# Attention's first rows in two halves, its output sums begun while probabilities are turned, routing steps spread, and the stages on either side reordered

## What is computed

```
x = x + gate * mamba(norm(x))        # layer 0: projections, a scan over 16 states, W_out
x = x + gate * moe8(norm(x))         # layer 0: 8 experts, the 2 best for each row
x = x + gate * attention(norm(x))    # layer 1: 8 heads of 128, causal softmax, T = 1024
x = x + gate * moe16(norm(x))        # layer 1: 16 experts, 2 best, at most 640 rows each

scores = q k^T / sqrt(128), masked; probs = softmax(scores)
out    = (probs v) for each head, times Wo, summed over the 8 heads
```

## Time and profile before

| | |
|---|---|
| time, 3 runs | 2908.6 us median, 2907.63 to 2910.3 |
| the profiled execution | 2909.66 us, span 2907.9 us |
| busy, share of the span | PE 86%, DVE 72%, ACT 45%, POOL 42% |
| idle time of PE in the attention steps | 31.9 us between 1405 and 2515 us |
| the chain that ended last | from the boundary at 2585.59 us, nearly all PE |

### The profile page before, as it was taken

One profiled execution on the slowest core, in us unless ns is written; L12 is line 12 of the kernel. 1 busy time (PEld: TensorE's weight loads), 2 busy tenths in 40 slices (PEclk: granted clock), 3 DMA queues, 4 the chain that ended last, 5 costly groups with the idle time before them and its releaser, 6 DMA issues. The chain is left out here.

```text
span 2907.9 us, 39192 instructions
## 1 busy us (share of the span) xinstructions
PE 2492.8 (86%) x12341; PEld 1792.0 (62%) x12342; DVE 2103.6 (72%) x4277; ACT 1296.4 (45%) x2563; POOL 1234.4 (42%) x531
## 2 busy tenths in 40 slices
PE   6677867868766759998799999999999999959998
PEld 4355545645545559998466666666666666647776
DVE  4999999999999566665666567766776677655554
ACT  4677677677665235554243324332433243311111
POOL 2799999999999036666000000020002000223344
PEclk8889989889986879999899999999999999969999
DMA  4645555555556254334300010001001000035554
GB/s 147 192 154 186 178 174 186 176 171 192 165 180 206 81 173 64 64 63 61 114 1 1 1 48 1 1 31 34 1 1 34 15 1 1 30 112 128 129 130 74
DMA packets 150845, 268.98 MB, mean 92 GB/s; under 512 B 18316, under 2 KB 107324, under 8 KB 150172
## 3 DMA queue, kind: packets, MB, share of 16 engines
q1 hardware_dynamic: 121916, 227.12, 24.3%
q0 software_dynamic: 28224, 37.78, 7.7%
q10 hardware_dynamic: 544, 2.10, 0.2%
HBM read 209.52 MB, written 57.43 MB: 92 GB/s over the span
## 5 line engine op out<-in xcount | busy, mean ns | idle before, releaser
L765 POOL TENSOR_TENSOR dbx<-u,b_all 128x2048 f32<-128x2048 f32 x128 | 578.6, 4535 | 71.2 <-DVE u L844 33.3
L1805 POOL DMA_INDIRECT slots<-at_r_rows,slot_of x64 | 62.7, 980 | 1140.3 <-DVE slot_of L2220 1048.5
L649 ACT ACTIVATE da_ps<-delta,a_neg 128x512 f32<-128x512 f32 x512 | 347.9, 689 | 132.7 <-DVE hc L917 124.5
L2066 ACT COPY at_pt<-at_pt_ps 128x512 f32<-128x512 f32 (+3 forms) x384 | 171.7, 483 | 504.5 <-PE at_pt_ps L1935 501.1
L469 PE MATMUL y_ps<-ident,hc 128*128 128x128 f32 x1536 | 246.5, 305 | 87.6 <-DVE hc L917 87.0
L1924 PE MATMUL at_s_ps<-at_qk 128*128 128x512 f32 (+3 forms) x768 | 291.4, 489 | 3.1 <-DVE at_v L2269 3.1
L1948 PE MATMUL at_o_ps<-at_pt,at_v 128*128 128x512 f32 (+3 forms) x768 | 288.6, 487 | 0.3 <-issue 0.3
L469 PEld LDWEIGHTS y_ps<-ident,hc 128*128 128x128 f32 x1536 | 200.6, 158 | 143.0 <-DVE hc L917 115.4
L2055 ACT ACTIVATE at_probs<-at_s_ps,at_small 128x128 f32<-128x128 f32 (+7 forms) x256 | 192.2, 751 | 202.2 <-DVE at_small L2280 198.9
L917 DVE TENSOR_TENSOR hc<-da_ps,c_all 128x512 f32<-128x512 f32 x384 | 257.7, 673 | 0.0
L907 DVE TENSOR_TENSOR_SCAN da_ps<-da_ps,state,dbx 128x512 f32<-128x512 f32 x192 | 243.4, 1277 | 4.5 <-ACT da_ps L649 3.6
...
...
## 6 DMA issues: line engine op xcount, KB each, us to landing
b_all<-bc_rows SPq DMA_DIRECT2D x128, 512.0 KB, 4.4
c_all<-bc_rows SPq DMA_DIRECT2D x128, 512.0 KB, 5.1
e_w<-L_ffn_w SPq DMA_DIRECT2D x32, 512.0 KB, 5.5
...
e_xs<-slots SPq DMA_DIRECT2D x16, 650.0 KB, 7.1
...
sums<-x SPq DMA_DIRECT2D x8, 512.0 KB, 6.9
```

Source lines behind the costliest of these rows:

```text
L649: nc.scalar.activation(da_ps[s % RING_DA][:], delta[:, c % 2, m, :], ACT.Exp, scale=sh.a_neg[:, m, n:n + 1]).then_inc(S["da_ready"], 1)
L765: nc.gpsimd.tensor_tensor(dbx[:, at % RING_DBX], pair, rows, ALU.mult).then_inc(S["dbx_ready"], 1)
L2066: nc.scalar.copy(pt[i // CT][:, half * CT:half * CT + m, at], pt_ps[half][:, 0:m, :]).then_inc(S[f"copied{half}"], 1)
```

## The change

1. **Scan.** The last chunk's output sums go to the freed banks da_ps[0] and [1]. Identity and the first two of four products of row tile 0 and 1 are put behind steps 61 and 62 of 64, those of tiles 2 and 3 behind the last `turn_back`. Behind POOL's gate two products a tile are left.
2. **Start of attention.** The first sequence's mods (256 KB) are loaded first, then both halves of x and `more`. All other loads wait until these have landed. DVE adds the first half in one instruction, POOL the second. Statistics, variance, root and rows are done for tiles 0 to 3 and then for 4 to 7. PE turns 4 tiles through two banks (`qk_ps`, `o_ps`), makes the three pieces of the first half, turns the other 4 tiles, and makes the other three pieces. PE waits for w_o, gate_w and the constants only at the end of the first batch.
3. **Every batch.** The pieces of head 0 come in the order q, k, v of the first half, then of the second. A bank waits for the output tile that used it, not for all eight. score(0) waits for five pieces, the sixth is awaited at step 4. The products over heads 0 to 6 of output tiles 0 and 1 are put into steps N and N + 1, ahead of turn(62) and turn(63); head 7 is added where the sums stood.
4. **Routing and next rows.** Weights move to step 50, ranks stay in 53, `slots` is parted: 5 instructions in step 54, 8 in 55. NORM moves from 53 to 55, so rows are normalised in steps 55 to 62; PE still turns them in 56 to 63. POOL's scatter is paced one step later.
5. **End of attention.** `w_qkv` is free once the last piece is made. The gates and the weights of experts 0 and 1 (2.5 MB) are loaded into its place then. `phase_experts1` starts with `e_xs` of expert 0, waits until it has landed, and loads that of expert 1.

Lines that were added or taken away, with common indentation removed and declarations left out:

```diff
@@ -481,6 +481,29 @@
+def last_first_blocks(j):
+    pair, i = j // 2, j % 2
+    if i == 0:
+        pe.wait_ge(S["hc_ready"], hc_at(LAST, STEPS - RING_DA + pair) + 1)
+        pe.wait_ge(S["y_gated"], LAST * HALVES + 1)
+        pe.wait_ge(S["w_ready"], B)
+    out = da_ps[pair][:, i * E:(i + 1) * E]
+    nc.tensor.matmul(out, sh.ident[:], sh.x[:, LAST * CT + j, :], start=(i == 0), stop=False, skip_group_check=True)
+    for k in range(2):
+        nc.tensor.matmul(out, u[:, LAST % 2, k, j * P:(j + 1) * P], sh.w_out[:, k, :], start=False, stop=False, skip_group_check=True)
+def last_blocks(pair):
+    if pair == 0:
+        pe.wait_ge(S["y_gated"], CHUNKS * HALVES)
+    for i in range(2):
+        j = pair * 2 + i
+        for k in range(2, MD):
+            mm = nc.tensor.matmul(da_ps[pair][:, i * E:(i + 1) * E], u[:, LAST % 2, k, j * P:(j + 1) * P], sh.w_out[:, k, :],
+                                  start=False, stop=(k == MD - 1), skip_group_check=True)
+    mm.then_inc(S["out_done"], 1)
@@ -500,6 +523,8 @@
+if c == LAST and k >= STEPS - 3 and k < STEPS - 1:
+    last_first_blocks(k - STEPS + 3)
@@ -524,9 +549,11 @@
-    turn_back(CHUNKS - 1, m)
+    turn_back(LAST, m)
+for j in range(2, CT):
+    last_first_blocks(j)
-    out_product(CHUNKS - 1, pair)
+    last_blocks(pair)
@@ -664,7 +691,8 @@
-nc.scalar.copy(sh.x[:, tile:tile + 2, :], proj_ps[pair][:].rearrange("p (i e) -> p i e", i=2)).then_inc(S["out_added"], 1)
+bank = da_ps[pair] if c == CHUNKS - 1 else proj_ps[pair]
+nc.scalar.copy(sh.x[:, tile:tile + 2, :], bank[:].rearrange("p (i e) -> p i e", i=2)).then_inc(S["out_added"], 1)
@@ -1498,15 +1525,14 @@
-sp.dma_start(sh.mods[:, 2], d["mod_rows"][1, 5].partition_broadcast(P)).then_inc(mods_in, 16)
-    if not early(e, 2):
-        sp.wait_ge(y_done, (e - 1) * S1)
+    if early(e, 2):
+        return
+    sp.wait_ge(y_done, (e - 1) * S1)
@@ -1516,6 +1542,7 @@
+sp.wait_ge(x_in[0], 16)
@@ -1723,8 +1751,8 @@
-SLOTS = (RANK, RANK + 1, RANK + 2)
-NORM, TURN, COPY = N - 11, N - 8, N - 7
+SLOTS = (RANK - 2, RANK + 1, RANK + 2, RANK + 3)
+NORM, TURN, COPY = N - 9, N - 8, N - 7
@@ -1735,13 +1763,16 @@
+sp.dma_start(sh.mods[:, 0:2, 0, :], d["mod_rows"][1, 0:2, 0].partition_broadcast(P)).then_inc(S["mods0_in"], 16)
-load_mods(sp, d, sh, 1, 0, S["mods_in"])
+sp.wait_ge(x_first[1], 32)
+sp.dma_start(pos[:], d["posT"]).then_inc(S["pos_in"], 16)
+sp.dma_start(sh.mods[:, 0:2, 1:B, :], d["mod_rows"][1, 0:2, 1:B].partition_broadcast(P)).then_inc(S["mods_in"], 16)
+sp.dma_start(sh.mods[:, 2], d["mod_rows"][1, 2].partition_broadcast(P)).then_inc(S["mods_in"], 16)
-sp.dma_start(pos[:], d["posT"]).then_inc(S["pos_in"], 16)
@@ -1767,8 +1798,17 @@
+sp.wait_ge(S["qk_done"], B * HEADS * PIECES + 1)
+sp.dma_start(sh.gates[:], d["mod_rows"][1, 5].partition_broadcast(P)).then_inc(sh.gates_in, 16)
+for e in range(2):
+    sp.dma_start(sh.w1[:, e], d["L1_ffn_w1"][e].rearrange("(k p) f -> p k f", p=P)).then_inc(sh.w1_in[e], 16)
+    sp.dma_start(sh.w2[:, e], d["L1_ffn_w2"][e].rearrange("(m p) f -> p m f", p=P)).then_inc(sh.w2_in[e], 16)
+sp.wait_ge(sh.gates_in, 16)
+for e in range(2):
+    sp.wait_ge(sh.w1_in[e], 16)
+    sp.wait_ge(sh.w2_in[e], 16)
@@ -1795,12 +1835,16 @@
+pool.wait_ge(x_first[1], 32)
+nc.gpsimd.tensor_tensor(sh.x[:, late], sh.x[:, late], more[:, late], ALU.add).then_inc(first_summed[1], 1)
-            pool.wait_ge(S["scored"], (rb + 1) * N + SLOTS[2] + 1 + j)
+            pool.wait_ge(S["scored"], (rb + 1) * N + SLOTS[3] + 1 + j)
@@ -1817,9 +1861,12 @@
+FIRST_PIECES = (0, 2, 4, 1, 3, 5)
+first_turned = (qk_ps, o_ps)
-    return qk_ps[:] if h else bank(i)
+    return qk_ps[:] if h else bank(FIRST_PIECES.index(i))
@@ -1828,15 +1875,19 @@
-pe.wait_ge(S["w_o_in"], 16)
-    pe.wait_ge(S["h_copied"], nb * TPB + j + 1)
+    out = qk_ps
+    if isinstance(nb, int) and nb == 0:
+        out = first_turned[j % 2]
+        pe.wait_ge(S["h_copied"], max(j, 1))
+    else:
+        pe.wait_ge(S["h_copied"], nb * TPB + j + 1)
-        last = nc.tensor.transpose(qk_ps[:, k * P:(k + 1) * P], rows[:, j % 4, k * P:(k + 1) * P], sh.ident[:])
+        last = nc.tensor.transpose(out[:, k * P:(k + 1) * P], rows[:, j % 4, k * P:(k + 1) * P], sh.ident[:])
@@ -1890,19 +1941,27 @@
-pe.wait_ge(S["gate_in"], 16)
-pe.wait_ge(S["consts_ready"], 12)
-for j in range(TPB):
+for j in range(CT):
-        if h > 0:
+        if h > 1 or i > 0:
-        elif i >= 4:
-            pe.wait_ge(S["qk_ready"], b * (HEADS * PIECES) + i - 2)
+        else:
+            pe.wait_ge(S["qk_ready"], b * (HEADS * PIECES) + h * PIECES + i)
+        products(h, i, out)
+    def project_first(place):
+        if place >= 4:
+            pe.wait_ge(S["qk_ready"], b * (HEADS * PIECES) + place - 2)
+        elif not first_batch:
+            pe.wait_ge(S["out_added"], b * TPB + place - 2)
+        products(0, FIRST_PIECES[place], bank(place))
+    def products(h, i, out):
@@ -1916,7 +1975,9 @@
-    pe.wait_ge(S["qk_ready"], b * (HEADS * PIECES) + h * PIECES + (4 if h else PIECES) + 1)
+    pe.wait_ge(S["qk_ready"], b * (HEADS * PIECES) + h * PIECES + (4 if h else PIECES - 1) + 1)
+if n == CT:
+    pe.wait_ge(S["qk_ready"], b * (HEADS * PIECES) + PIECES + 1)
@@ -1949,18 +2010,24 @@
-def output(t):
+def output(t, heads=range(HEADS)):
-    for h in range(HEADS):
+    for h in heads:
-    last.then_inc(S["out_done"], 1)
+    if HEADS - 1 in heads:
+        last.then_inc(S["out_done"], 1)
+if first_batch:
+    pe.wait_ge(S["h_copied"], CT + 1)
+    for place in range(PIECES // 2):
+        project_first(place)
+    for j in range(CT, TPB):
+        turn_rows(0, j)
-pe.wait_ge(S["out_added"], b * TPB + 1)
-for i in range(PIECES):
-    project(0, i)
+for place in range(PIECES // 2 if first_batch else 0, PIECES):
+    project_first(place)
@@ -1970,6 +2037,14 @@
+if n >= N:
+    if n == N:
+        if first_batch:
+            pe.wait_ge(S["w_o_in"], 16)
+            pe.wait_ge(S["gate_in"], 16)
+            pe.wait_ge(S["consts_ready"], 12)
+        pe.wait_ge(S["exp_done"], b * N + N - 1)
+    output(n - N, range(HEADS - 1))
@@ -1992,9 +2067,8 @@
-    pe.wait_ge(S["exp_done"], b * N + N - 1)
-output(t)
+output(t, range(HEADS - 1, HEADS))
@@ -2038,11 +2112,17 @@
+    turned = first_turned[j % 2] if isinstance(nb, int) and nb == 0 else qk_ps
-                   qk_ps[:, 0:KE * P].rearrange("p (k t) -> p k t", k=KE)).then_inc(S["h_copied"], 1)
-root(0)
-for j in range(TPB):
+                   turned[:, 0:KE * P].rearrange("p (k t) -> p k t", k=KE)).then_inc(S["h_copied"], 1)
+act.wait_ge(S["first_var"], 1)
+nc.scalar.activation(sh.var[:, 0:CT], sh.var[:, 0:CT], ACT.Sqrt).then_inc(S["first_std"], 1)
+for j in range(CT):
+    copy_rows(0, j)
+act.wait_ge(S["var_ready"], 1)
+nc.scalar.activation(sh.var[:, CT:TPB], sh.var[:, CT:TPB], ACT.Sqrt).then_inc(S["std_ready"], 1)
+for j in range(CT, TPB):
@@ -2205,15 +2282,20 @@
+def slot_sums(rb, k):
+    v = nc.vector
+    for source, dst in ((cand, slot), (rank, valid)):
+        linked(rb, v.tensor_tensor(scores[:], mask[:, k], source[:], ALU.mult))
+        linked(rb, v.tensor_reduce(dst[:, k], scores[:], AX_X, ALU.add))
+def slots_begun(rb):
+    dve.wait_ge(S["rank_taken"], rb + 1)
+    linked(rb, nc.vector.tensor_tensor(cand[:], rank[:], offs[:].rearrange("p (o e) -> p o e", o=1).broadcast_to([P, TPB, NE]), ALU.add))
+    slot_sums(rb, 0)
-    dve.wait_ge(S["rank_taken"], rb + 1)
-    linked(rb, v.tensor_tensor(cand[:], rank[:], offs[:].rearrange("p (o e) -> p o e", o=1).broadcast_to([P, TPB, NE]), ALU.add))
-    for k in range(2):
-        for source, dst in ((cand, slot), (rank, valid)):
-            linked(rb, v.tensor_tensor(scores[:], mask[:, k], source[:], ALU.mult))
-            linked(rb, v.tensor_reduce(dst[:, k], scores[:], AX_X, ALU.add))
+    slot_sums(rb, 1)
@@ -2245,20 +2327,46 @@
-for j in range(TPB):
-    stats(0, j)
-variance(0)
-invert(0)
-dve.wait_ge(S["mods_in"], 16)
-for j in range(TPB):
-    normalise_rows(0, j)
+early = slice(0, CT)
+dve.wait_ge(x_first[0], 32)
+nc.vector.tensor_tensor(sh.x[:, early], sh.x[:, early], more[:, early], ALU.add).then_inc(first_summed[0], 1)
+first_link = link_on(dve, S["first_chain"])
+def first_rows(th, var_ready, std_ready, rstd_ready):
+    dve.wait_ge(first_summed[th], 1)
+    at = slice(th * CT, (th + 1) * CT)
+    for j in range(th * CT, (th + 1) * CT):
+        nc.vector.bn_stats(sh.stats[:, j, :], sh.x[:, j, :]).then_inc(S["stats_in"], 1)
+    dve.wait_ge(S["stats_in"], (th + 1) * CT)
+    first_link(nc.vector.tensor_tensor(mean, stat(1), stat(4), ALU.add))
+    nc.vector.scalar_tensor_tensor(out=var, in0=var, scalar=1.0 / E, in1=dif, op0=ALU.mult, op1=ALU.add).then_inc(S[var_ready], 1)
+    dve.wait_ge(S[std_ready], 1)
+    nc.vector.reciprocal(sh.rstd[:, at], sh.var[:, at]).then_inc(S[rstd_ready], 1)
+    dve.wait_ge(S[rstd_ready], 1)
+    if th == 0:
+        dve.wait_ge(S["mods0_in"], 16)
+    for j in range(th * CT, (th + 1) * CT):
+        normalise_rows(0, j)
```

(22 more changed lines are left out.)

31 lines of the change are left out of this document (19 added, 12 removed).

## The result

The changed kernel takes 2878.87 us (median of 4 runs, 2877.21 to 2879.94) against 2909.22 us of the kernel before beside it (2907.63 to 2910.3). The ratio is 0.9896, 95% interval 0.9878 to 0.9913: 30.3 us faster. The profiled execution has a span of 2878.2 us, 29.7 less than before.

A forecast was written before the change was run, and what follows sets the result against it. PE was taken as the bound, busy 86% of the span, so time is won only where it idles or runs at half clock. 6.9 + 7.1 + 8.6 + 4.3 + 2.2 = 29.1 us off 2909.66; forecast 2880, range 2873 to 2891.

The forecast's parts named there:

- the filled hole: Scan's end: PE's 3.1 us without work ahead of POOL's gate would be filled up to some 0.6 us.
- the full clock: Scan's end: the 16 instructions behind POOL's gate run at full clock, 3.5 us; half clock would cost 3.5 more.
- rival of half clock: Half clock behind the scan's gate and at attention's start, price 3.5 + 2.6 us: 2886; chance 0.17.
- some 0.7 us: Attention's start: time for loading 256 KB of mods first, at 350 to 400 GB/s, so DVE starts at 1385.0.
- some 2.3: Attention's start: DVE's variance stands still beside POOL's add; without that contention the sum has 2.3 us less.
- (a): Batch end: early output sums cover PE's wait of 1.11 or 1.33 us for probabilities, 4.7 in all.
- (b): Between batches: a bank waits only for its own output tile, so 1.6 us of PE waiting goes.
- (c): Batch start: score(0) no longer waits for v; three more waits of 0.78 us go, 2.3.
- Left: 0.7: Routing, step 55: of PE's wait for v, then for probabilities 54, 0.7 us stays; gain 1.9 twice.
- second rival: Waits move on instead of going: routing's steps give 1.5 us, the per-batch changes 5.5, total 2886; chance 0.15.
- wrong if PE's idle time in attention stays above 20 us: Attention: the prediction's own sign of failure; PE's idle time there was 31.9 us before.

The follow-up runs named there:

- experiment 4: Changed kernel with the scan's last four output tiles made whole behind POOL's last gate, as before the change: 2884.9 us, ratio 0.9922 to the kernel before.
- experiment 3: Changed kernel with output sums of tiles 0 and 1 made whole behind the last step, as before the change: 2884.3 us, ratio 0.9924 to the kernel before.
- experiment 8: Changed kernel with two waits put back: first piece for all outputs of the previous batch, score(0) for v: 2886.9 us, ratio 0.9923 to the kernel before.
- experiment 2: Changed kernel with routing's steps as before: weights, ranks and slots in steps 52 to 54, rows from 53: 2882.9 us, ratio 0.9917 to the kernel before.
- experiment 6: Changed kernel with batch 0's mods (256 KB) loaded behind the first half's x and more: 2879.4 us, ratio 0.9899 to the kernel before.
- experiment 9: Changed kernel with the second half's add by DVE and batch 0's mods loaded behind the first half: 2873.9 us, ratio 0.9887 to the kernel before.
- experiment 11: Changed kernel with add by DVE, mods second, middle batches' slots in step 65 and scatters spread over the next batch: 2870.4 us, ratio 0.9873.
- experiment 1: Changed kernel with the add for the second half of attention's first rows by DVE, not POOL: 2875.6 us, ratio 0.9894 to the kernel before.
- experiment 5: Changed kernel with slots of the middle batches moved from steps 54 and 55 to step 65: 2881.5 us, ratio 0.9904 to the kernel before.
- experiment 10: Changed kernel with middle batches' slots in step 65 and their scatters held back to steps 8 to 15 of the next batch: 2873.2 us, ratio 0.9884.
- experiment 7: Changed kernel without the wait that holds back expert 1's rows until expert 0's have landed: 2878.9 us, ratio 0.9897 to the kernel before.

## Why the prediction was right

The time came at 2878.9, forecast 2880. That it came so near is in part luck: three parts were too large, two too small, and part 4 won its time by another way than was forecast. The parts (us):

| part | predicted | found | by |
|---|---|---|---|
| 1 scan's end | 6.9 | 6.1 to 6.2 | the traces, experiment 4 |
| 2 attention's start | 7.1 | 6.5 | the traces |
| 3 each batch | 8.6 | 5.6 + 5.8, less about 0.9 counted in part 2 | experiments 3, 8 |
| 4 routing | 4.3 | 2.6 | experiment 2 |
| 5 layer 1's experts | 2.2 | 2.5 | PE's first turning after the stage's start, 6.87 before, 4.37 after |

The column sums to 28.2 and the spans differ by 29.7; the 1.5 between is within the spread of equal code.

**Part 1** went as worked out, step by step: the filled hole, the full clock, 0.23 an instruction where 0.216 was taken. The rival of half clock did not occur.

**Part 2** was right but for one term. DVE began 7.7 us after the stage's start instead of 6.65: the "some 0.7 us" for the mods' 256 KB were mis-sized, the add starts 1.5 to 1.9 us earlier with the mods behind it (experiments 6, 9, 11). Of that, 1.2 reaches score(0) in experiment 6 and 0.3 between experiments 1 and 9; the rest went into first pieces that took longer there (6.54 and 6.02 us). The stall beside POOL's add came in the variance as forecast, 2.16 against "some 2.3"; without it score(0) comes 2.8 earlier (experiment 1).

**Part 3** was too small. The idle time was near: 4.3 against 4.7 for (a), and 4.9 for the waits of (b) and (c) that experiment 8 brought back. Two terms were put at nothing. The first is the restart. Where PE need not wait, its next group starts about 0.17 us before the modelled end of the last: the output group of batch 0 runs 1647.58 + 20.89 = 1668.47, and the piece starts at 1668.30; with a wait it starts after that end (experiment 8). The group behind a wait is also 0.09 or 0.10 longer, 3.69 against 3.60 for the piece and 0.92 against 0.82 for score(0). Eleven waits went, at 0.27 each some 3.0 us that the idle column does not hold. The second term takes some back: the five new waits. The 0.49 of batch 2 costs 0.85, for its first piece is 11.29 us ahead of score(0) and 10.44 in batches 1 and 3; the four at head 1 cost little, score(0) to that piece is 3.51 us in batch 0 and 3.42 in experiment 8. As an estimate from these numbers, 9.2 + 3.0 - 0.85 makes 11.3; the two experiments have 11.4, each within about 0.9. The Trainium skill, page "TensorE: Matmul & The Clock Gate", section "Step-by-step: what each phase is for", has the draining of one product overlap the filling of the next; the trace agrees in kind, with 0.17 us.

**Part 4** was right in its gain only roughly, and wrong in its mechanism. The step that failed is "Left: 0.7": I followed DVE no further than the probabilities that PE turns in step 56. That wait came at 1.51, and in step 57 another of 1.12 followed, because the work taken out of steps 53 and 54 was still ahead of both. In the two middle batches PE waits 5.2 us in these steps before and after; 3.8 us less were forecast. That is the second rival's mechanism, in full. What was won there against the kernel before is the clock: its waits of 2.61 and 2.62 were followed by stretches at 0.64 and 0.63, and the piece and the turning behind took 1.75 us longer (3.03 + 1.49 against 1.95 + 0.82 in batch 1). Behind the two shorter waits, with work between them, the clock stayed at 1.00. Experiment 2 shows this in batch 1 alone; in batch 2 its order costs 1.0 of idle time, so the 2.6 are clock and idle time both. I had costed those rows' slow piece nowhere, though 3.03 stood in the earlier trace rows. Experiments 5 and 10 show that the waits are DVE's backlog: with 3.9 us of work moved away only 0.66 is left.

**Part 5** came as worked out from the transfer. The wait added before the second load, which I took for harmless, is so (experiment 7).

My own test "wrong if PE's idle time in attention stays above 20 us" struck: it stayed at 23.5, where the sum wanted some 18. It struck with reason. The 3.8 us of the middle batches did not go, and 1.9 us of new short waits came. The time came all the same, because two things that the prediction had priced nowhere, the restart behind each wait and the slow instructions behind a long one, made up for it.
